# Softplus of a Mamba block: two VectorE intermediates move from PSUM to SBUF, and two operations change places

## The reference, cut to what matters

```python
dt = jnp.einsum('blr,dr->bdl', dt_r, dt_proj_w)
dt = jax.nn.softplus(dt + dt_bias[None, :, None])
...
def step(h, inp):
    x_t, dt_t, B_t, C_t = inp
    dA = jnp.exp(dt_t[..., None] * A)
    dBx = dt_t[..., None] * B_t[:, None, :] * x_t[..., None]
    h = dA * h + dBx
    y = jnp.einsum('bdn,bn->bd', h, C_t)
    return (h, y)
```

## Time and profile before

| what | value |
|---|---|
| time of the runs, median (lowest to highest of 3) | 3049.44 us (3047.0 to 3049.85) |
| profiled execution, from the first to the last instruction | 3047.5 us |
| busy, share of the span | PE 93%, DVE 79%, POOL 56%, ACT 52% |
| softplus stage, first DVE operation to the end of the last | 236.9 to 318.3 us |

### The profile page before, as it was taken

How to read it: one execution, slowest core, us unless ns; L and a number is a source line. 1 busy time by engine, 2 the same in 40 slices (tenths; PEclk the granted TensorE clock), 3 DMA queues, 4 the chain that set the end, 5 groups by cost and what they waited for, 6 DMA issues and landing times. The chain is left out here.

```text
span 3047.5 us, 35696 instructions
## 1 busy us (share of the span) xinstructions
PE 2833.3 (93%) x11958; PEld 2028.4 (67%) x11958; DVE 2393.1 (79%) x2168; ACT 1574.6 (52%) x2685; POOL 1712.8 (56%) x1035
## 2 busy tenths in 40 slices
PE   8997588888788889999999999999989999999997
PEld 7882244444222348888888888887768888887886
DVE  6558999999999977444777777765988888885677
ACT  4448555555665545213888888873433333334443
POOL 0003999999999953403888888861044444430034
PEclk9995799999999999999999999999989999999999
DMA  4228886666875645232111111215245555567654
GB/s 152 83 83 261 274 200 159 179 171 152 250 219 148 199 150 216 104 119 72 37 37 37 37 37 37 71 54 200 97 156 180 180 179 180 180 218 238 194 176 139
DMA packets 217641, 445.84 MB, mean 146 GB/s; under 512 B 33661, under 2 KB 47741, under 8 KB 215613
## 3 DMA queue, kind: packets, MB, share of 16 engines
q1 hardware_dynamic: 179742, 390.73, 41.1%
q10 hardware_dynamic: 37728, 52.96, 5.3%
HBM read 313.45 MB, written 130.15 MB: 146 GB/s over the span
## 5 line engine op out<-in xcount | busy, mean ns | idle before, releaser
L1927 POOL TENSOR_TENSOR at_p_lo<-at_p,at_p_hi 128x512 fp32r<-128x512 f32 x384 | 514.6, 1348 | 244.3 <-ACT at_p_hi L1820 236.5
L716 POOL TENSOR_TENSOR scan_dbx<-scan_u,scan_b_bc 128x1024 f32<-128x1024 f32 x256 | 596.1, 2359 | 0.0
L885 ACT ACTIVATE mamba_ps<-scan_dt,scan_a_neg 128x512 f32<-128x512 f32 (+1 forms) x512 | 332.0, 680 | 315.1 <-DVE scan_g L903 291.3
L914 DVE TENSOR_TENSOR_SCAN mamba_ps<-mamba_ps,scan_dbx 128x1024 f32<-128x1024 f32 x195 | 440.0, 2283 | 3.1 <-ACT mamba_ps L887 1.7
L1847 DVE TENSOR_REDUCE at_neg_max<-heads_ps 128x1 fp32r<-128x1536 f32 x128 | 224.9, 1757 | 134.4 <-PE heads_ps L1939 132.4
L108 PE MATMUL heads_ps<-ff_x_hi,ff_w_hi 128*128 128x512 f32 x784 | 310.0, 395 | 17.2 <-DVE ff_u L2572 6.4
L2812 POOL TENSOR_TENSOR ff_raw<-ff_raw,ff_scale 128x512 f32<-128x512 f32 x112 | 115.9, 1066 | 361.2 <-DMA ff_raw<-in_w 252.8
L109 PE MATMUL heads_ps<-ff_x_lo,ff_w_hi 128*128 128x512 f32 x784 | 308.1, 393 | 0.0
L110 PE MATMUL heads_ps<-ff_x_hi,ff_w_lo 128*128 128x512 f32 x784 | 308.1, 393 | 0.0
L1816 ACT ACTIVATE at_p<-heads_ps 128x512 f32<-128x512 f32 x384 | 228.2, 594 | 110.0 <-PE heads_ps L1963 95.8
L1820 ACT ACTIVATE at_p_hi<-at_p 128x512 fp32r<-128x512 f32 x384 | 242.8, 632 | 12.2
(11 more groups left out here) (306 smaller groups left out, 6906.8 us busy)
## 6 DMA issues: line engine op xcount, KB each, us to landing
scan_dt<-dt SPq DMA_DIRECT2D x120, 256.0 KB, 4.8
scan_u<-u SPq DMA_DIRECT2D x120, 256.0 KB, 7.6
ff_raw<-in_w SPq DMA_DIRECT2D x56, 512.0 KB, 4.6
ff_down_ar<-ac SPq DMA_DIRECT2D x98, 256.0 KB, 2.8
ff_down_hr<-hc SPq DMA_DIRECT2D x98, 256.0 KB, 2.7
ff_act_w<-in_w SPq DMA_DIRECT2D x14, 1024.0 KB, 7.6
hc<-ff_act_t SPq DMA_DIRECT2D x56, 256.0 KB, 6.2
ac<-ff_act_v SPq DMA_DIRECT2D x56, 256.0 KB, 5.9
```

What stands on the lines that cost most here:

```text
L716: nc.gpsimd.tensor_tensor(dbx[n % SL][:].rearrange("p (h l) -> p h l", h=2), u[it % 2][:, c:c + 2], b_bc[b][:, k // 2].unsqueeze(1).to_bro ...
L885: nc.scalar.activation(at[:, h * L + h:(h + 1) * L], dt[it % 2][:, c, h:L], ACT.Exp, scale=a_neg[:, it % IT, e:e + 1]).then_inc(a_ready, 1)
L914: nc.vector.tensor_tensor_scan(out[:], ps_a[n % SA], dbx[n % SL][:], 0.0, ALU.mult, ALU.add).then_inc(scanned, 1)
L1927: nc.gpsimd.tensor_tensor(p_lo[n % NSL][:], p[n % NSL][:], f32(p_hi[n % NSL][:]), ALU.subtract).then_inc(p_lo_done, 1)
```

## The change

The place `ps_t` in PSUM is given up. `t` = (e + 1) - 1 and then c = e - t are written in SBUF, to `dd`. The ramp plus the logarithm is written over the logarithm, in `ll`, and the last operation adds `dd` and `ll`. The c operation comes ahead of the r operation. The waits follow the buffers: `t` needs `dd` free and so takes the waits for the store and for POOL's product of tile i - 4, it no longer waits for dt of the tile before; the logarithm waits until dt of tile i - 4 has read `ll`.

```diff
-    ps_x, ps_t = [ps_dt[0], ps_dt[1], ps[0]], ps[1]
+    ps_x = [ps_dt[0], ps_dt[1], ps[0]]
...
             if i >= ND:
                 act.wait_ge(c_done, i - ND + 1)
+                act.wait_ge(l_done, i - ND + 1)
...
         def logarithm(i):
             act.wait_ge(e_done, i + 1)
             if i >= ND:
-                act.wait_ge(r_done, i - ND + 1)
+                act.wait_ge(dt_done, i - ND + 1)
...
         for i in range(IT):
             dve.wait_ge(e_done, i + 1)
-            dve.wait_ge(dt_done, i)
-            nc.vector.tensor_scalar(ps_t, ee[i % ND][:], 1.0, -1.0, ALU.add, ALU.add).then_inc(t_done, 1)
-            dve.wait_ge(l_done, i + 1)
             if i >= ND:
                 dve.wait_ge(dt_st[i % ND], 16 * (i // ND))
                 dve.wait_ge(u_done, i - ND + 1)
-            nc.vector.scalar_tensor_tensor(dd[i % ND][:], ps_x[i % 3], 0.0, ll[i % ND][:],
+            nc.vector.tensor_scalar(dd[i % ND][:], ee[i % ND][:], 1.0, -1.0, ALU.add, ALU.add).then_inc(t_done, 1)
+            dve.wait_ge(t_done, i + 1)
+            nc.vector.tensor_tensor(dd[i % ND][:], ee[i % ND][:], dd[i % ND][:], ALU.subtract).then_inc(c_done, 1)
+            dve.wait_ge(l_done, i + 1)
+            nc.vector.scalar_tensor_tensor(ll[i % ND][:], ps_x[i % 3], 0.0, ll[i % ND][:],
                                            ALU.max, ALU.add).then_inc(r_done, 1)
-            dve.wait_ge(t_done, i + 1)
-            nc.vector.tensor_tensor(ps_t, ee[i % ND][:], ps_t, ALU.subtract).then_inc(c_done, 1)
             dve.wait_ge(c_done, i + 1)
             dve.wait_ge(r_done, i + 1)
-            nc.vector.tensor_tensor(dd[i % ND][:], dd[i % ND][:], ps_t, ALU.add).then_inc(dt_done, 1)
+            nc.vector.tensor_tensor(dd[i % ND][:], dd[i % ND][:], ll[i % ND][:], ALU.add).then_inc(dt_done, 1)
```

## The result

The changed kernel takes 3067.04 us (median of 4 runs, 3065.39 to 3070.7), against 3048.65 us for the kernel before (4 runs, 3047.0 to 3049.85): 18.4 us more, a ratio of 1.006 with a 95% interval of 1.0046 to 1.0074. The profiled execution took 3068.17 us, with a span of 3066.8 us.

What follows compares the result with a forecast made beforehand. DVE bounds the softplus stage, busy 56.49 of 58.20 us. Tiles of 6.25 us instead of 4.85 give +19.4, with the scan's products +19.6: span 3047.5 becomes 3067.1, plus 1.9 for the median 3069.0; range 3063 to 3076.

Steps and rivals of the forecast that it cites:

- (a): Softplus stage: POOL gets its turn before `t` in each tile, +1.75 us a tile, total 3075; chance 0.07.
- (b): Softplus stage: `t` stays at 1.23 us and takes no turn of its own, +14.5 us, total 3064; chance 0.05.
- (c): Softplus stage: c, 0.03 us behind `t`, keeps POOL out, about +5 us, total 3054; chance 0.04.
- (d): Softplus stage: DVE and POOL don't block each other, ACT's 4.39 us a tile limits, 7.5 us less, 3042; chance 0.04.
- the ring: Softplus stage, seen in e1, not forecast: r, PE, ACT, then r two tiles later; 9.60 us for two tiles.
- the main case: Softplus stage: POOL's product runs between `t` and c, a tile takes 6.25 us instead of 4.85, total 3069; chance 0.80.

Runs made afterwards that it cites:

- e1: Changed kernel with POOL's product in the softplus stage cut to one column (work left out): 3046.63 us, ratio 0.9989 to the kernel before.
- e2: Changed kernel with `t` alone put back into PSUM, the order of the change kept: 3049.09 us, ratio 0.9999 to the kernel before.
- e5: Changed kernel with POOL's product of a tile waiting for c of the next tile: 3059.7 us, ratio 1.0032 to the kernel before.
- e6: Changed kernel with POOL's product replaced by a memset that writes but reads nothing (work left out): 3046.82 us in its one run.
- e3: Changed kernel with r put back between `t` and c, all in SBUF: 3055.08 us, ratio 1.0019 to the kernel before.
- e9: Changed kernel with the freed PSUM place as a fourth place for x, POOL's product whole: 3068.91 us, ratio 1.0073 to the kernel before.
- e7: As e1 (product cut, work left out), with the freed PSUM place as a fourth place for x: 3040.57 us, ratio 0.9976 to the kernel before.
- e4: Changed kernel with the order of before and `t` in PSUM, but c and dt in SBUF: 3049.83 us, ratio 1.0003 to the kernel before.

## Why the prediction was right, and where it was not

**The mechanism.** The step that the prediction rests on, c with two SBUF inputs behind a `t` that lets POOL in, held in each part: forecast 0.68 us for `t`, 3.26 for c, 1.22 for r and dt, 2.7 for POOL's product, against 0.687, 3.246, 1.211, 1.226 and 2.722. e1 and e2 take the wait away from two sides (no long POOL operation; no second SBUF input), e5 moves it to another instruction, and in e6 a POOL operation that only writes doesn't hold c up. That the wait comes from both engines reading SBUF, and not from the in-place writing or from c standing directly behind `t`, is shown. The order sets how much of the wait is covered: with r ahead of c it is 1.0 us of c's time and not 2.0 (e3).

**The tile.** Forecast 6.25 us, measured 6.35. The missing 0.10 is almost all ahead of dt. I took the 0.03 us at which dt follows c before; now dt follows r, and it starts 0.11 us behind it (r runs from 301.46 + 3.25 - 0.08 = 304.63 to 305.84, dt starts at 305.95). In e2, where nothing waits for POOL, the same step takes 0.10. Over the 13 tiles from 2 to 14 this is 1.3 us; in the last tile dt waits for POOL anyway, and its end came 7.17 us behind that of the tile before, as forecast.

**The ends.** In the first two tiles `t` of tile 1 waited for POOL (2.25 us) and cost nothing, since r waits for ACT's logarithm there, as said. The last dt was forecast near 2.1 and took 2.05.

**The sum.** Forecast +19.4 us up to the scan's first operation, measured +20.8; the total +19.6 forecast, +19.3 in the profiles, +18.4 by the medians. In the profiles the path can be followed: the first `t` starts 0.6 us later, the stage takes 20.8 more, 0.7 are added up to the last split of `ff_hs` on DVE, which comes 22.1 us later (3032.94 against 3010.86), and the end of the program gives 2.8 back. From that split to the end, the profiled execution of before takes 36.6 us and that of the changed kernel 33.9. In the matmuls there the granted clock is 0.84 (a mean of the two levels) and 1.00, the upper level (windows of the two kernels, columns as in the earlier trace rows):

```profile
3027.50:3038.00 10.50, 9.53 (x35) 7.18 (x33) 7.14 (x17) 6.01 (x18) 1.70 (x3) 0.84 0.03 11
```
```profile
3048.40:3057.40 9.00, 7.89 (x35) 5.99 (x33) 7.05 (x17) 6.15 (x18) 2.20 (x4) 1.00 0.11 40
```

The instructions there are the same in all kernels of this study, and the stretch took 32.6 to 36.7 us in their ten profiles, with 36.7, 35.4 and 33.9 among the kernels at 4.8 to 5.4 us a tile, and 35.4 in e9, whose tiles take as long as those of the changed kernel. So I count it as scatter of the end and not as an effect of the change, though each kernel has only one profile; what sets the clock there in one execution and not in another stays open. That the total came out closer than the stage is luck: the stage was forecast 1.4 us too short, and the end gave more than that back.

**The rivals.** (a), POOL ahead of `t`, happened once, in tile 1. (b), `t` unchanged at 1.23, is out by 0.687. (c), c keeps POOL out, is out by 3.25. (d), no blocking, is out, and it was also mis-sized: "ACT with 4.39 becomes the limit" is wrong. A tile can't take less than the ring's 4.80 us with three PSUM places, so the most that (d) could have given was 14 x 0.05 + 1.1, about 2 us, and not 7.5. (e1's 2.6 us less are not a measure of it, since they come from POOL's missing product; e7, with the ring opened, shows the stage at 76.0 us against 81.3.) The error didn't touch the forecast, since the main case lies above the ring, but it did touch what I expected of e1 and e4.

No version here beats the kernel before with all its work in it. The four-place version needs the place of `t`, and `t` outside PSUM brings the turns with POOL.

## What to carry to other kernels

Ask of each VectorE operation how many of its inputs lie in SBUF, and what GpSimd runs beside it: a PSUM operand can be what lets the two engines run side by side, and `t` at 1.2 us in PSUM was cheaper than `t` at 0.7 us in SBUF with a neighbour that waits 2 us. Where the two must meet, put an operation with at most one SBUF input into GpSimd's turn; e3 got back two thirds of the loss with that alone. And where work is left out to test a wait, look where the time is gained: e1's gain lay behind the stage that it was meant to test. Before an engine's busy time per step is called the next limit, follow one buffer around: r, matmul, ACT and r again took 9.60 us for two tiles, and no engine's busy time shows it.

## What the hardware showed that I had not expected

- A wait for the other engine's turn doesn't appear as idle time but inside the instruction (c at 3.25 us instead of 1.22, in 14 of 16 tiles), and the profile names no releaser for it.
- An operation that was held ends 1.08 us (c, 1024 elements) behind the end of POOL's, though it takes 1.22 alone, and POOL's product ends 2.19 us behind `t`, though it takes 2.35. So about 0.15 us of each of these two overlaps the other engine's turn. With e6's memset, which reads nothing, it is 0.05 us: it ends 0.89 us behind `t` (271.10 against 270.21) and takes 0.94 alone.
- How far a dependent DVE operation starts behind the one that it waits for is not one number: 0.03 us for c behind `t` and, before, for dt behind c, but 0.10 to 0.11 us for dt behind r, and 0.10 in the kernel before for `t` behind dt, which is a TENSOR_TENSOR like c. No run here isolates what makes the difference.
